# A three-layer graph attention network on one core: the high and low float16 halves of two tiles transposed by one DMA each instead of two

## What is computed

```python
h = jnp.maximum(_layernorm(x), 0.0)
x = x + gnn(h, adj, ...)
# gnn, for each layer l:
si, sj = x @ attn_w[l, :d], x @ attn_w[l, d:]
scores = leaky(si[:, :, None] + sj[:, None, :] + attn_b[l], 0.2)
attn = softmax(where(adj + eye > 0, scores, -inf))
h = layernorm(x + attn @ x, g1[l], beta1[l])
ff = gelu(h @ W1[l] + b1[l]) @ W2[l] + b2[l]
x = layernorm(h + ff, g2[l], beta2[l])
```

## Time and profile before

| | us |
|---|---|
| three runs | 2242.72, 2245.41, 2245.51 |
| median | 2245.41 |
| profiled execution, its own time | 2242.66 |
| its span in the profile | 2240.5 |
| TensorE matmuls busy | 2195.1 (98%) |
| POOL, ACT, DVE busy | 1908.8 (85%), 1885.0 (84%), 1875.0 (84%) |
| DMA queue of SP (q1), share of the 16 engines' time | 27.0% |
| mean granted TensorE clock | 0.997 |

### The profile page before, as it was taken

How to read it: one execution, slowest core, us unless ns; L and a number is a source line. 1 busy time by engine, 2 the same in 40 slices (tenths; PEclk the granted TensorE clock), 3 DMA queues, 4 the chain that set the end, 5 groups by cost and what they waited for, 6 DMA issues and landing times.

```text
span 2240.5 us, 46173 instructions
## 1 busy us (share of the span) xinstructions
PE 2195.1 (98%) x15464; PEld 1524.0 (68%) x15464; DVE 1875.0 (84%) x5886; ACT 1885.0 (84%) x3496; POOL 1908.8 (85%) x1644
## 2 busy tenths in 40 slices
PE   4999999999999999999999999999999999999998
PEld 3666766766666666676666666676666666667665
DVE  7889797888998787878999878787899978787864
ACT  6888888889998888888999888888899988888874
POOL 5888788889998888889999888888999888888886
PEclk9999999999999999999999999999999999999999
DMA  6522212145552112113655121213455211211253
GB/s 148 130 70 53 58 32 41 32 67 95 110 115 53 39 34 39 34 39 72 123 97 111 36 41 32 41 32 50 79 114 121 48 39 34 39 34 39 53 95 66
DMA packets 382266, 144.71 MB, mean 65 GB/s; under 512 B 312144, under 2 KB 380368, under 8 KB 382032
## 3 DMA queue, kind: packets, MB, share of 16 engines
q1 hardware_dynamic: 366192, 126.04, 27.0%
q0 software_dynamic: 15840, 15.73, 5.0%
HBM read 49.96 MB, written 16.78 MB: 30 GB/s over the span
## 4 chain that ended last, share of the span: by engine, by line
PE 90%; DVE 7%; issue 1%; ACT 1%; POOL 1%; DMA 0%; DVEq 0%; POOLq 0%; ACTq 0%
PE p_hid L459 41%; PE p_pair L473 41%; PE p_pair L511 5%; PE p_pair L497 2%; DVE bn L719 1%; DVE g_lo L712 1%; DVE dots L757 1%; DVE res L795 1%; DVE dots L760 1%; DVE p_lo L807 1%; DVE adj_in L740 0%; PE p_pair L484 0%; DVE mv L724 0%; POOL rstd L984 0%; DMA x_in<-in_x 0%
## 5 line engine op out<-in xcount | busy, mean ns | idle before, releaser
L473 PE MATMUL p_pair<-w_hi,g_hi 128*128 128x256 f16 x3072 | 838.0, 273 | 0.0
L473 PE MATMUL p_pair<-w_lo,g_hi 128*128 128x256 f16 x3072 | 838.0, 273 | 0.0
L473 PE MATMUL p_pair<-w_hi,g_lo 128*128 128x256 f16 x3072 | 837.9, 273 | 0.0
L577 ACT ACTIVATE p_hid<-p_hid,b_eff 128x512 f32<-128x512 f32 x768 | 503.1, 655 | 274.7 <-PE p_hid L459 273.5
L712 DVE TENSOR_TENSOR g_lo<-p_hid,g_hi 128x512 f16<-128x512 f32 x768 | 517.1, 682 | 45.8 <-ACT g_hi L582 38.4
L582 ACT ACTIVATE g_hi<-p_hid 128x512 f16<-128x512 f32 x768 | 458.5, 597 | 24.3
L459 PE MATMUL p_hid<-hT_hi,w_hi 128*128 128x512 f16 x1536 | 458.4, 380 | 14.4 <-DVE g_lo L712 10.6
L459 PE MATMUL p_hid<-hT_lo,w_hi 128*128 128x512 f16 x1536 | 458.2, 380 | 1.1 <-DMA hT_lo<-h_lo 1.1
L459 PE MATMUL p_hid<-hT_hi,w_lo 128*128 128x512 f16 x1536 | 458.2, 380 | 0.0
L473 PEld LDWEIGHTS p_pair<-w_lo,g_hi 128*128 128x128 f16 x3072 | 300.8, 98 | 106.7 <-issue 0.3
L473 PEld LDWEIGHTS p_pair<-w_hi,g_hi 128*128 128x128 f16 x3072 | 300.8, 98 | 106.6 <-issue 0.3
(11 more groups left out here) (77 smaller groups left out, 3565.3 us busy)
## 6 DMA issues: line engine op xcount, KB each, us to landing
out<-w_f SPq DMA_DIRECT2D x31, 512.0 KB, 4.8
x_in<-in_x SPq DMA_DIRECT2D x30, 512.0 KB, 4.6
w_f<-in_x POOLq DMA_DIRECT2D x30, 512.0 KB, 6.9
adj_in<-in_adj SPq DMA_DIRECT2D x32, 256.0 KB, 5.7
w_f<-in_L_gnn_W SPq DMA_DIRECT2D x6, 1024.0 KB, 7.4
hT_hi<-h_hi SPq DMA_TRANSPOSE x96, 3.1
hT_lo<-h_lo SPq DMA_TRANSPOSE x96, 3.1
pT_hi<-p_hi SPq DMA_TRANSPOSE x94, 2.4
```

The lines of the kernel that those rows point to most:

```text
L473: mm = pe.matmul(ff_banks(s)[:, t, :], g[i][:, nodes], w[l][:, c, :], start=(c == 0 and t % 2 == 0 and n == 0), stop=(c == C - 1 and n == ...
L577: act.activation(p_hid[k][:], p_hid[k][:], ACT.Gelu, bias=b1_eff[:, l, c:c + 1], scale=1.0 / WSCALE).then_inc(gelu_ready, 1)
```

## The change

The high and the low half of a tile become two parts of one tensor (`h_both`, `hT_both`, `p_both`, `pT_both`, with the half as the first index behind the partition), and the old names become views of them, so that every engine reads and writes the same shapes as before. SP turns both halves with one DMA, of 16 blocks of 128 x 128 for the rows and of 8 for the probabilities, after both halves are written. The transpose of the rows stands where that of the low half stood, behind the load of `x`; that of the probabilities waits for p_hi, for the aggregation before it and for p_lo. TensorE waits for the one semaphore ahead of the first matmul of chunk 0. Whoever waited until a half had been transposed before he overwrites it now waits for the transpose of both. For the first two items, `pT_hi_ready` is left as a semaphore between ACT and DVE.

```diff
-        p_hi, p_lo = sb("p_hi", [P, T, N], F16), sb("p_lo", [P, T, N], F16)
-        pT_hi, pT_lo = sb("pT_hi", [P, T, N], F16), sb("pT_lo", [P, T, N], F16)
+        p_both, pT_both = sb("p_both", [P, 2, T, N], F16), sb("pT_both", [P, 2, T, N], F16)
+        p_hi, p_lo, pT_hi, pT_lo = p_both[:, 0], p_both[:, 1], pT_both[:, 0], pT_both[:, 1]
...
+        h_both = sb("h_both", [P, 2, T, D], F16)
+        h_hi, h_lo = h_both[:, 0], h_both[:, 1]
+        hT_both = [sb(f"hT_both{i}", [P, 2, T, KD, N], F16) for i in range(2)]
+        hT_hi, hT_lo = [b[:, 0] for b in hT_both], [b[:, 1] for b in hT_both]
...
-            def turn_h_hi(r, s):
+            def turn_h(r, s):
                 if later(r, s, 2):
                     sp.wait_ge(hid_psum, total(r, s - 2, C, C))
                 sp.wait_ge(h_hi_ready, total(r, s, 1, 1))
-                sp.dma_start_transpose(hT_hi[s % 2][:].rearrange("p t k n -> p (t k) n"),
-                                       h_hi[:].rearrange("p t d -> p (t d)")).then_inc(hT_hi_ready, 16)
-
-            def turn_h_lo(r, s):
                 sp.wait_ge(h_lo_ready, total(r, s, 1, 1))
-                sp.dma_start_transpose(hT_lo[s % 2][:].rearrange("p t k n -> p (t k) n"),
-                                       h_lo[:].rearrange("p t d -> p (t d)")).then_inc(hT_lo_ready, 16)
+                sp.dma_start_transpose(hT_both[s % 2][:].rearrange("p h t k n -> p (h t k) n"),
+                                       h_both[:].rearrange("p h t d -> p (h t d)")).then_inc(hT_ready, 16)
...
+            def turn_probs(r, s):
                 sp.wait_ge(p_hi_ready, total(r, s, 1, -1))
                 if later(r, s):
                     sp.wait_ge(agg_ready, total(r, s - 1, 1, 1))
...
                 sp.wait_ge(p_lo_ready, total(r, s, 1, -1))
...
+                sp.dma_start_transpose(pT_both[:].rearrange("p h t n -> p (h t) n"),
+                                       p_both[:].rearrange("p h t n -> p (h t n)")).then_inc(pT_ready, 16)
...
             def slot(r, s):
                 if is_item(r, s + 2):
-                    turn_probs_hi(r, s + 2)
-                    turn_probs_lo(r, s + 2)
+                    turn_probs(r, s + 2)
...
-                if is_item(r, s + 1):
-                    turn_h_hi(r, s + 1)
...
                 if is_item(r, s + 1):
-                    turn_h_lo(r, s + 1)
+                    turn_h(r, s + 1)
...
                 if c == 0:
-                    pe.wait_ge(hT_hi_ready, total(r, s, 16, 16))
+                    pe.wait_ge(hT_ready, total(r, s, 16, 16))
...
-                    if c == 0 and n == 2 * KD:
-                        pe.wait_ge(hT_lo_ready, total(r, s, 16, 16))
...
             def aggregate(r, s):
-                pe.wait_ge(pT_hi_ready, total(r, s, 16, 16))
-                pe.wait_ge(pT_lo_ready, total(r, s, 16, 16))
+                pe.wait_ge(pT_ready, total(r, s, 16, 16))
```

More of the change, by code:

```diff
@@ L194, in gnn_kernel @@
         h_res = [sb(f"h_res{i}", [P, T, D]) for i in range(2)]
-        h_hi, h_lo = sb("h_hi", [P, T, D], F16), sb("h_lo", [P, T, D], F16)
-        hT_hi = [sb(f"hT_hi{i}", [P, T, KD, N], F16) for i in range(2)]
-        hT_lo = [sb(f"hT_lo{i}", [P, T, KD, N], F16) for i in range(2)]
+        h_both = sb("h_both", [P, 2, T, D], F16)
+        h_hi, h_lo = h_both[:, 0], h_both[:, 1]
+        hT_both = [sb(f"hT_both{i}", [P, 2, T, KD, N], F16) for i in range(2)]
+        hT_hi, hT_lo = [b[:, 0] for b in hT_both], [b[:, 1] for b in hT_both]
         g_hi = [sb(f"g_hi{i}", [P, TN], F16) for i in range(GS_RING)]
@@ L263, in gnn_kernel @@
         pT_hi_ready = sem("pT_hi_ready")
-        pT_lo_ready = sem("pT_lo_ready")
+        pT_ready = sem("pT_ready")
         X_hi_ready = sem("X_hi_ready")
@@ L273, in gnn_kernel @@
         h_lo_ready = sem("h_lo_ready")
-        hT_hi_ready = sem("hT_hi_ready")
-        hT_lo_ready = sem("hT_lo_ready")
+        hT_ready = sem("hT_ready")
         h_res_steps = sem("h_res_steps")
@@ L427, in opening @@
                 next_adj(4)
-                turn_h_hi(0, 0)
-                turn_h_lo(0, 0)
+                turn_h(0, 0)
                 for dst, v in ((g2_rows, g2), (beta2_rows, beta2)):
@@ L624, in copy_probs @@
                     act.wait_ge(agg_ready, i)
-                act.activation(pT_hi[:], first_pT(i), ACT.Copy).then_inc(pT_hi_ready, 16)
+                act.activation(pT_hi, first_pT(i), ACT.Copy).then_inc(pT_hi_ready, 1)
             def high_probs(r, s):
@@ L629, in high_probs @@
                 if later(r, s):
-                    act.wait_ge(pT_hi_ready, total(r, s - 1, 16, 16))
-                act.activation(p_hi[:], probs[:], ACT.Copy).then_inc(p_hi_ready, 1)
+                    act.wait_ge(pT_ready, total(r, s - 1, 16, 16))
+                act.activation(p_hi, probs[:], ACT.Copy).then_inc(p_hi_ready, 1)
             def high_X(r, s):
@@ L644, in high_h @@
                 if later(r, s):
-                    act.wait_ge(hT_hi_ready, total(r, s - 1, 16, 16))
-                act.activation(h_hi[:], norm1[:], ACT.Copy).then_inc(h_hi_ready, 1)
+                    act.wait_ge(hT_ready, total(r, s - 1, 16, 16))
+                act.activation(h_hi, norm1[:], ACT.Copy).then_inc(h_hi_ready, 1)
             def slot(r, s):
@@ L805, in low_probs @@
                 if later(r, s):
-                    dve.wait_ge(pT_lo_ready, total(r, s - 1, 16, 16))
-                dve.tensor_tensor(p_lo[:], probs[:], p_hi[:], ALU.subtract).then_inc(p_lo_ready, 1)
+                    dve.wait_ge(pT_ready, total(r, s - 1, 16, 16))
+                dve.tensor_tensor(p_lo, probs[:], p_hi, ALU.subtract).then_inc(p_lo_ready, 1)
             def first_low_probs(i):
-                dve.wait_ge(pT_hi_ready, 16 * i + 16)
+                dve.wait_ge(pT_hi_ready, i + 1)
                 if i:
                     dve.wait_ge(agg_ready, i)
-                dve.tensor_tensor(pT_lo[:], first_pT(i), pT_hi[:], ALU.subtract).then_inc(pT_lo_ready, 16)
+                dve.tensor_tensor(pT_lo, first_pT(i), pT_hi, ALU.subtract).then_inc(pT_ready, 16)
             def residual_rows(layers):
@@ L1000, in low_h @@
                 if later(r, s):
-                    pool.wait_ge(hT_lo_ready, total(r, s - 1, 16, 16))
-                pool.tensor_tensor(h_lo[:], norm1[:], h_hi[:], ALU.subtract).then_inc(h_lo_ready, 1)
+                    pool.wait_ge(hT_ready, total(r, s - 1, 16, 16))
+                pool.tensor_tensor(h_lo, norm1[:], h_hi, ALU.subtract).then_inc(h_lo_ready, 1)
             def low_X(r, s):
```

6 lines of the change are left out of this document (removed).

## The result

The changed kernel takes 2246.49 us (median of 20 runs, 2245.76 to 2250.35); the kernel before, timed beside it, 2244.36 us (20 runs, 2242.49 to 2245.94). The ratio is 1.0014, with a 95% interval of 1.0007 to 1.0020. It is not simply that of the two medians: these lie 2.13 us or 0.09% apart, the two means 2.96 us, the two lowest runs 3.27 us. The profiled execution took 2247.04 us, with a span of 2244.9.

The account below looks back on a forecast made before the run. TensorE, busy 2195.1 of 2240.5 us, sets the pace. Profiled 2242.7 us + 2.35 (opening) + 0.8 (loading slots) + 0 (quiet slots) = 2245.8, plus 2.75 for the median: 2248.5 us, 0.14% more; range 2243 to 2257.

Parts of the forecast that it names:

- The price of the double transpose: SP's DMA transposes: 16 blocks land 4.35 us after issue and hold SP some 1.3 us; 8 blocks land after 3.05.
- Quiet slots: Some 80 mid-run slots: the rows' transpose lands with 3.9 us of cover left, so cost 0.
- The opening: Start of the run, nothing covers the landing: first matmul near 40.5 us, cost 2.35 us, bounds 0.8 and 5.6.
- the case that the prediction had priced at 1.65: Opening: the clock rises at the same moment as today, the second chunk runs partly at full clock, delay 1.65 us.
- sign of 1.6 to 3 us: Opening: the end of the first g_lo wait comes 1.6 to 3 us later than 53.02, if the forecast is right.
- The loading slots: 15 slots loading new graphs, DMA engines full: rows land d = 0.3 us later, cost 0.8 us, bounds 0 and 14.
- The slower rival: Loading slots: second 8 blocks don't overlap the load of x, d 1.3 us or more, 2255.0 us; chance 0.32.
- The better rival: Loading slots: fewer, larger transfers pay, TensorE's 0.4 us g_lo waits go, at most 4.7 us, 2243.1 us; chance 0.10.
- The split form: A 16-block transpose is carried out as two of 8, all terms stay, 2248.5 us; chance 0.55 together with the forecast.

Follow-up runs that it names:

- the wide fold: Bias fold's one-column matmuls made 64 equal columns wide, one of them read: 2242.41 us on the kernel before, 2245.00 us on the changed kernel.
- e2: Kernel before with only the rows' two transposes merged into one DMA, the probabilities left apart: 2246.30 us, ratio 1.0012.
- e4: Kernel before, nothing merged, both row transposes issued back to back once both halves are written, TensorE waiting for both before chunk 0: 2246.50 us, ratio 1.0013.
- e5: Kernel before with only item 0's two row transposes issued late, TensorE waiting for both before its first matmul: 2246.98 us, ratio 1.0016.
- e6: Changed kernel with the rows' transpose issued ahead of the load of x in SP's list: 2246.34 us, ratio 1.0011.
- e1: Kernel before with only the probabilities' transposes merged into one DMA, the rows left apart: 2242.83 us, ratio 0.9998.
- e3: Changed kernel with item 0's rows turned by two DMAs instead of one: 2244.41 us, ratio 1.0002.
- e8: Changed kernel with TensorE's opening reordered, item 1's probabilities transposed ahead of chunk 0, spread of s_j and aggregation ahead of chunk 1: 2244.84 us, ratio 1.0003.
- e10: Changed kernel with the bias fold's one-column matmuls made 64 columns wide: 2245.00 us, ratio 1.0009.
- e7: Kernel before with TensorE's opening reordered, item 1's probabilities transposed between chunk 0's high and low matmuls, spread and aggregation ahead of chunk 1: 2241.11 us, ratio 0.9989.
- e12: Changed kernel with item 0's rows turned by two DMAs, rows' transpose ahead of the load of x, and 64-column bias fold: 2242.31 us, ratio 0.9993.

## Why the prediction was right

The forecast was 3.15 us or 0.14% more than before. The medians lie 2.13 us apart, the means 2.96, the lowest runs 3.27, and with the wide fold, whose profiles have no half-clock stretch behind a fold, the medians lie 2.6 us apart. The direction and the two places were foreseen; that the ratio of 1.0014 agrees to the last digit is in part luck, since it holds clock stretches for which the prediction had no term. The 2248.5 us are 2.0 us above the median that came out; 1.05 us of that is the base, for the median of before was 2245.4 in three runs, two of which were of the upper group, and 2244.4 in twenty, where it falls between the groups. By steps:

- **The price of the double transpose** held: 4.3 us for 4.35, 3.1 for 3.05. The Trainium skill's figure, from which the prediction estimated 3.2 us, is in "DMA: Bandwidth & Descriptors", Anatomy of one DMA, a fit for DMAs issued from GpSimd; these are transposes issued from SP, so the 4.3 us say that it does not carry over to them, and nothing on the figure where it belongs. SP's time to issue the transpose was mis-sized: 1.75 to 1.97 us in quiet slots instead of 1.3, and 3.9 to 6.1 in loading slots. In quiet slots nothing waits behind it.
- **Quiet slots** cost nothing, as said: 22.59 us and full. The transpose issued at 1003.50 landed 3.9 us ahead of the slot's start at 1011.72, which is the cover that the prediction computed.
- **The opening** was predicted at 2.35 us. Comparing the profiles with item 0 late (the changed kernel, e2, e4, e5, e6: slot 1 at 71.3 to 72.1, mean 71.7) with those where it is not (before, e1, e3: 69.6 to 70.3, mean 69.9) gives 1.8 us at the start of slot 1 and 2.1 us at the start of slot 2. The first matmul came at 40.69 (40.5 predicted), the delay at the transposes of the probabilities was 3.17 us (3.05 predicted), and the clock, which rose at about 44 us in both, gave part of it back in the second chunk, the case that the prediction had priced at 1.65. 0.46 us more came back between the spread of s_j, 1.86 us late, and chunk 3, 1.40 us late. That is just outside the sign of 1.6 to 3 us that the prediction had given for this place. It had no term for the transpose of item 1, for which TensorE waits 0.42 us at the start of slot 1 in this profile and 0.43 in e2's; no other profile lists such a wait.
- **The loading slots** were predicted at 0.8 us for a landing d = 0.3 us later (the margins as listed add up to 0.9), and 1.2 were measured in the changed kernel's profile. The mechanism is as said: the load of x now goes 0.03 us after the normalised input is done, where it went up to 2 us later, and the transpose follows earlier. What it half missed is the size of the 4 blocks of probabilities that move into the burst. It took them to disappear for the most part; e1 shows that by themselves they make the rows land about 1 us later, and the changed kernel against e2 0.45 us. The two movements nearly cancel: the mean margin of the 15 slots is 0.90 us where it was 1.02. E2 without the merged probabilities has no loss there, e1's 0.3 us are the one late start of 0.25 us, and both together behind the load of x have 0.6 to 1.6 us over before (the changed kernel, e3, e8, e10).
- **The slower rival** (7 to 14 us in the loading slots) is out: waits come in two of 15 slots, 0.55 us together, and not in most. **The better rival** is out: the holes of 0.4 us before g_lo stayed in every second loading slot: the waits for g_lo behind the opening are 11.2 - 5.9 = 5.3 us, where they were 10.6 - 5.9 = 4.7 before. **The split form** is not decided: the trace shows one issue and one landing a transpose, and 4.3 us fits it (1.23 + 3.05) as well as the single form. Both have the same price here, so nothing hangs on it.
- **What the prediction did not have** is the clock behind the folds. It gave the clock a part in the opening alone. It is worth 1.7 us a stretch. With one profile of each kernel, whether executions of the changed kernel meet such a stretch more often than those of before, and why they would, stays open. The moment of the fold may matter (the five profiles in which item 0 is late and the rest of the opening as it was all have a stretch; before and e1 have none, but e3 has two and e7, whose opening is earlier, has one), but nothing was run to test that.

The rule of the Trainium skill that would have made the change a gain ("DMA: Bandwidth & Descriptors", Rules for kernel authors: coalesce many small transfers) did not show: 94 DMAs less in e1 and 189 less in e12 are worth nothing that the runs can tell. The rule says that it is below 64 KB that one pays mostly overhead, and the halves joined here are of 128 and 256 KB, so the runs do not speak against it. Another line of the same section, issue a DMA early and wait for it late, is the one that the trace agrees with: e4 breaks it without merging, and its median of 2246.50 us is that of the changed kernel.

## What to carry to other kernels

Joining two DMAs makes the earlier one as late as the later one's data. Before doing it, look for the places in which nothing covers the landing: the first item, whose wait stands at the head of a chain, and the stages where the DMA engines are full; the steady state, where a transfer has microseconds of cover (3.9 us here), gives neither gain nor loss. A hundred joined transfers that nobody waited for are worth nothing, while three lines in another order on the waiting engine (e7) were worth 2.4 us; and where run times fall in groups, read the granted clock in short windows before explaining a difference smaller than the distance of the groups.

## What was not expected of the hardware

- TensorE's clock fell here although the profile shows TensorE idle for no more than 0.26 us at a time. In the window 229 to 231 us it is 1.81 of 2 us busy, mostly with one-column float32 matmuls, and the clock granted behind it is 0.67, then 0.50. With 64 columns no profile of four has such a stretch and the second group of run times is gone, at 0.1 us for a fold. So a busy TensorE in the profile is no sign by itself that the clock will stay up.
- The time that SP needs to issue a transpose is longer where the DMA engines have other transfers to do: the 16-block one took 1.75 to 1.97 us in quiet slots and 5.99 in a loading slot, the two of 8 blocks before 3.6 and 1.6. It hid behind other work here, since nothing urgent was listed behind it.
